# Four-layer transformer block: context maxima, spline stage, last FFN0 stage, ScalarE's order and FFN1's token transposition changed together

## The reference

```python
x = x + tanh(g_xattn[0]) * mlstm(layernorm(x), ctx, ctx, Wi, bi, Wf, bf, ln_scale)   # 16 heads of 32
x = x + tanh(g_ffn[0])   * spline_ffn(layernorm(x), gate_cp, up_cp, down_cp)          # 2048 hidden
x = x + tanh(g_xattn[1]) * attention(layernorm(x), ctx, ctx)                          # 8 heads, over channels
x = x + tanh(g_ffn[1])   * mx_ffn(layernorm(x), gate_w, up_w, down_w)                 # 2048 hidden
```

## Time and profile before

| what | value |
|---|---|
| median of three runs | 1443.43 us |
| the profiled execution's own time | 1442.51 us |
| its span from the first to the last instruction | 1440.4 us |
| TensorE's mean granted clock | 0.932 of full speed |
| busy: PE, DVE, ACT, POOL | 1246.8, 1157.2, 584.2, 367.5 us |
| spline stage, DVE busy / length | 51.4 / 77.1 us |
| FFN0 stages, PE busy / length | 232.3 / 260.5 us |
| FFN1, PE busy / length | 511.4 / 525.4 us |

### The profile page before, as it was taken

One profiled execution on the slowest core, in us unless ns is written; L12 is line 12 of the kernel. 1 busy time (PEld: TensorE's weight loads), 2 busy tenths in 40 slices (PEclk: granted clock), 3 DMA queues, 4 the chain that ended last, 5 costly groups with the idle time before them and its releaser, 6 DMA issues. The chain is left out here.

```text
span 1440.4 us, 18200 instructions
## 1 busy us (share of the span) xinstructions
PE 1246.8 (87%) x6611; PEld 597.2 (41%) x6635; DVE 1157.2 (80%) x1541; ACT 584.2 (41%) x963; POOL 367.5 (26%) x294
## 2 busy tenths in 40 slices
PE   4579999556899898887787888889999999999998
PEld 3258778431343343333122222244444444444444
DVE  6557788875888888888768777888899888889986
ACT  3344665345544444452455645322222322322222
POOL 0031433355433323310367597400000000000000
PEclk8879999675899999998799989999999999999999
DMA  8511033145734263232402304462111121211121
GB/s 292 176 65 61 11 118 118 57 135 179 206 100 135 88 176 88 82 114 83 117 1 64 68 16 87 96 126 51 37 36 36 40 47 39 55 36 36 37 45 44
DMA packets 166561, 122.43 MB, mean 85 GB/s; under 512 B 123855, under 2 KB 134759, under 8 KB 166364
## 3 DMA queue, kind: packets, MB, share of 16 engines
q1 hardware_dynamic: 165212, 117.34, 30.5%
q0 software_dynamic: 1280, 4.20, 1.0%
HBM read 61.15 MB, written 27.66 MB: 62 GB/s over the span
## 5 line engine op out<-in xcount | busy, mean ns | idle before, releaser
L1858 PE MATMUL FD<-W1H,HH 128*128 128x512 f16 x512 | 157.7, 390 | 6.7 <-DVE ROOM L1920 3.6
L2769 PE MATMUL HD<-W1H,HT 128*128 128x512 f16 x480 | 146.5, 382 | 2.5 <-DMA HT<-OS 2.5
L1774 POOL TENSOR_TENSOR HL<-ROOM,HH 128x512 f16<-128x512 f32 x48 | 74.2, 1546 | 168.1 <-ACT HH L1797 168.1
L1852 PE MATMUL FG<-W1L,W1H 97*128 97x512 f16 x324 | 84.3, 385 | 31.9 <-DVE ROOM L1920 14.0
L2534 DVE TENSOR_REDUCE NQ<-A_M 128x2 f32<-128x1024 f32 x60 | 73.3, 1222 | 36.1 <-PE A_M L2382 35.9
L2693 ACT CAST OS<-SS 128x2048 f16<-128x2048 f32 x14 | 26.6, 1899 | 183.9 <-DVEq L2858 183.9
L335 ACT ACTIVATE DD<-E,TM 128x128 f32<-128x128 f32 x256 | 72.9, 370 | 68.4 <-PE E L431 66.8
L1858 PE MATMUL FD<-W1H,HL 128*128 128x512 f16 x256 | 99.4, 388 | 0.0
L2334 ACT ACTIVATE PT<-A_S,CM 128x1024 f32<-128x1024 f32 x64 | 71.2, 1112 | 60.2 <-PE A_S L2408 60.1
L2769 PE MATMUL HD<-W1L,HT 128*128 128x512 f16 x240 | 91.6, 382 | 0.0
L2256 POOL TENSOR_TENSOR SS<-SS,PT 128x512 f32<-128x512 f32 x62 | 83.1, 1360 | 23.8 <-ACT PT L2334 11.3
(11 more groups left out here) (431 smaller groups left out, 2747.8 us busy)
## 6 DMA issues: line engine op xcount, KB each, us to landing
VALP<-in_ffn_weights_dram SPq DMA_DIRECT2D x24, 512.0 KB, 4.1
VALQ<-in_ffn_weights_dram SPq DMA_DIRECT2D x24, 512.0 KB, 4.4
quantised_weights<-QQ SPq DMA_DIRECT2D x24, 512.0 KB, 5.2
X<-in_x_dram SPq DMA_DIRECT2D x8, 1024.0 KB, 6.3
W1L<-features_kept SPq DMA_DIRECT2D x16, 288.0 KB
CTX<-in_ctx_dram SPq DMA_DIRECT2D x4, 1024.0 KB, 7.1
features_kept<-W1L SPq DMA_DIRECT2D x4, 1024.0 KB, 6.0
down_weights<-NAT SPq DMA_DIRECT2D x4, 1024.0 KB, 4.6
```

Source lines behind the costliest of these rows:

```text
L1774: pool.tensor_tensor(HL[:, KI - 1 - i, :], HM[:, i % 2, :], HH[:, i, :], ALU.subtract).then_inc(hl_ready, 1)
L1852: last = pe.matmul(banks[t][:, :], GW[rows, t, lhs, cols], F[b % 2][rows, rhs, c, :], start=(n == 0), stop=(n == 2))
L1858: last = pe.matmul(DN[c][:, :], lhs[:, at, c * P:(c + 1) * P], W2[:, i, part, :], start=(i == 0 and n == 0), stop=(i == KI - 1 and n == 2))
L2769: ins = pe.matmul(DN[:, :], HT[:, lp, i, :], W[:, 2, i * D:(i + 1) * D], start=(i == 0 and lp == 0 and W is WH), stop=(i == KI - 1 and lp ...
```

## The change

Five edits come together.

- **Context maxima.** VectorE reduces each context batch in the mLSTM phase's first loop, four instructions over 128x2048 into columns 3 to 6 of `MXQ`. The library operation that joins the weights' maxima takes seven columns instead of three. GpSimd clamps them afterwards with a `tensor_scalar`. All four batches' scales are formed by four small VectorE instructions at the start of FFN0 (`entry.scales`), and every `top`, `columns`, `largest`, `everywhere` and `scale` of FFN0 and the attention goes, with the three library operations of the attention.
- **Spline stage.** The clearing of `CT` is split between VectorE and GpSimd. ScalarE forms `ln` instead of GpSimd. The first eight units take their slots in `NAT` instead of `WF`, so that ScalarE waits for the added heads (`x_final`) only at unit 8. The units that turn features move from 8 to 11 to 10 to 13, the moments from 14 to 17 to 15 to 18, the last low part to VectorE. SP fetches batch 1's features in FFN0, behind the quantiser's first three loads.
- **FFN0's last stage.** The context is loaded as soon as the last hidden rows are ready, one quantiser tile earlier. The keys move from step 14 to 6 (ScalarE) and 9 (VectorE), batch 1's statistics to step 2, and the queries' low part to GpSimd.
- **ScalarE's order.** In steps that have both, `high` of tile n-1 goes ahead of `bound` of tile n.
- **FFN1.** From tile 3 on the tokens are turned by two transposing DMAs of 128x512 each (high and low part), which SP issues between the two of the hidden tile; TensorE's transpositions and ScalarE's copy of these 13 tiles go.

```diff
@@ spline_phase
-TURN_UNITS = (8, 9, 10, 11)
+TURN_UNITS = (10, 11, 12, 13)
+    def slot(u):
+        if u < CLASS_UNITS:
+            return NAT[0:rows(u), KI - 4 + u % 4, :, :].rearrange("p a d -> p (a d)").bitcast(F32)
+        return WF[0:rows(u), u % 4, :]
...
-                elif k == 8:
-                    features.keep_moments(sp, 1)
-            features.near_elements(sp, 1)
-            features.near_moments(sp, 1)
+            features.keep_moments(sp, 1)
...
-            pool.memset(CT[:, :, :], 0.0).then_inc(ct_zero, 1)
+            pool.memset(CT[:, 1, :], 0.0).then_inc(ct_zero, 1)
             heads = WF[:, :, :]
-            pool.wait_ge(ln_loaded, 16)
-            pool.tensor_scalar(ln, ln, tg[:, 0:1], -1.0, ALU.mult, ALU.mult).then_inc(x_scaled, 1)
...
-            act.wait_ge(x_final, 2)
             for u in range(UNITS_W):
+                if u == CLASS_UNITS:
+                    act.wait_ge(x_final, 2)
...
@@ WeightPeaks
+    def context(self, v, b, ctx):
+        v.tensor_reduce(self.MX[:, 3 + b:4 + b], ctx.rearrange("p c d -> p (c d)"), AX.X, ALU.max,
+                        apply_absolute_value=True).then_inc(self.ctx_max, 1)
...
+        pool.wait_ge(self.ctx_max, B)
         pool.wait_ge(self.mx_ready, 1)
         pool.partition_all_reduce(self.MXA[:, :], self.MX[:, :], P, RMAX).then_inc(self.all_max, 1)
+        pool.wait_ge(self.all_max, 1)
+        pool.tensor_scalar(self.MXA[:, :], self.MXA[:, :], 1e-30, None, ALU.max).then_inc(self.all_max, 1)
@@ FirstBatch
-    def low(self, v):
-        v.wait_ge(self.qh_ready, 1)
+    def low(self, pool):
+        pool.wait_ge(self.qh_ready, 1)
...
-ENTRY = {"deviation": 0, "inverse": 1, "queries": 2, "high": 4, "low": 5, "turn": (7, 9), "values": (8, 10),
-         "top": 11, "columns": 12, "everywhere": 13, "keys": 14}
+ENTRY = {"deviation": 0, "inverse": 1, "queries": 2, "high": 4, "low": 4, "turn": (7, 9), "values": (8, 10),
+         "keys": 6, "keys_low": 9, "statistics": 2}
@@ ffn0_phase
                 quantiser.load(sp, n)
+            features.near_elements(sp, 1)
+            features.near_moments(sp, 1)
...
-                    if s == STAGES - 1 and n == tiles[1]:
+                    if n == sum(STAGE_TILES[0:STAGES - 1]) - 1:
                         sp.wait_ge(hl_ready, B * KI)
...
                     for n in range(Q_TILES):
+                        if ROUNDED_STEP[n] + 1 == at:
+                            quantiser.high(act, n)
+                    for n in range(Q_TILES):
                         if EXPONENT_STEP[n] == at:
                             quantiser.bound(act, n)
-                    for n in range(Q_TILES):
-                        if ROUNDED_STEP[n] + 1 == at:
-                            quantiser.high(act, n)
@@ attention_phase
-                if step == 6 and g % 2 == 1 and b + 1 < B:
-                    scale(b + 1)
...
-            for part in range(2):
-                top(1, part)
-            scale(1)
...
-                if odd:
-                    scale(b + 1)
@@ ffn1_phase
+    PE_TURNED = 3
...
+                    if part == 0 and PE_TURNED <= tt + 2 < TILES:
+                        turned_tokens(tt + 2)
+
+            def turned_tokens(tt):
+                sp.wait_ge(gu_ready, (tt - 1) * IC)
+                for part, ready in enumerate((tokens.xh_ready, tokens.xl_ready)):
+                    sp.wait_ge(ready, tt + 1)
+                    sp.dma_start_transpose(out=XT[tt % 2][:, part, :, :], in_=tokens.XQ[:, part, :]).then_inc(xt_in, 16)
...
-                    pe.wait_ge(xt_taken, tt + 1)
+                    if isinstance(tt, int) and tt < PE_TURNED:
+                        pe.wait_ge(xt_taken, tt + 1)
+                    else:
+                        pe.wait_ge(xt_in, tt * 32 + 32 - 32 * PE_TURNED)
...
-                        if i == IC - 1 and more:
+                        if i == IC - 1 and isinstance(tt, int) and tt + 1 < PE_TURNED:
                             tokens.turn(pe, tt + 1, T[0][:, :, :, :])
```

More of the change, by code:

```diff
@@ L1129, in _ @@
                 t, g = divmod(j, INTER // SUB)
+                if j == 6:
+                    features.transposes(pe, 0, range(0, 2), T)
                 if j >= 6:
@@ L1183, in _ @@
                     features.norm(v, 0, range(NC))
+                    v.wait_ge(ct_zero, 1)
+                if j == 6:
+                    features.low(v, 0, range(0, 2), T)
                 v.wait_ge(ct_high, j + 1)
@@ L2695, in stage @@
                 if gate_up and more:
+                    if not (isinstance(tt, int) and tt + 1 <= PE_TURNED):
+                        act.wait_ge(xt_in, tt * 32 + 32 - 32 * PE_TURNED)
                     tokens.high(act, tt + 1)
                 silu(2)
-                if gate_up and more:
-                    tokens.turned(act, tt + 1, 1 - par, T[0][:, :, :, :])
                 silu(3)
```

187 lines of the change are left out of this document (76 added, 111 removed).

## The result

The changed kernel took 1423.72 us, the median of five runs between 1409.09 and 1424.89, beside 1445.28 us, the median of five runs of the kernel before: a ratio of 0.9845 with a 95% interval from 0.9814 to 0.9876. The forecast was 1410 us with a range from 1394 to 1432. The same kernel was timed twice more in the experiments, on two different chips, with 1412.76 us (0.9816, 0.9799 to 0.9833) and 1412.55 us (0.981, 0.9794 to 0.9826). One run of before, at 1466.53 us, lies outside its fast runs and is left out of the ratios.

The account below looks back on a forecast made before the run. No engine was taken to bound the whole kernel: TensorE bounds FFN1, other phases are largely waits. Terms 2.5 - 8.5 - 2.4 + 0.5 - 5 - 8.5 - 6 - 5.2 = -32.6 us from 1442.5 gave 1410 us, range 1394 to 1432.

Parts of the forecast that it names:

- mLSTM, +2.5: mLSTM phase: early context maxima on VectorE cost +1.5 us and GpSimd's clamp, stalled behind the library operation, +1.
- Spline stage, -8.5: Spline stage: start 4.7 us sooner without the wait for GpSimd's heads, and 3.6 of a 5.48 us wait (0 to -10.9).
- the zero end: Spline stage gains 0 if the loop waits for the heads at unit 8 as long as at unit 0.
- The boundary, -4.8 and +2.4: Batch 1's feature loads leave the spline-FFN0 boundary, -4.8 us; landing late in FFN0 gives half back, net -2.4.
- Scales, +0.5: FFN0's start: the four scale instructions cost +0.5 us (0 to +0.8).
- ScalarE's order, -5: FFN0's full stages: high ahead of bound returns a quarter of TensorE's 20.7 us of waits (+2 to -10).
- FFN0's last stage, -8.5: TensorE loses its context waits, VectorE sets the stage at 53.0 us: -9.5, 1 given back to clock (-4 to -14).
- the 58 that I had named as a sign of being wrong: FFN0's last stage: a length staying above 58 us would show the forecast wrong.
- Attention, -6: Attention: three batches' maxima leave VectorE and 39 us of stalls leave GpSimd, giving -6 us (-1 to -12).
- FFN1, -5.2: FFN1: turning 13 tiles' tokens by DMA instead of TensorE gives net -5.2 us (-5.9 to +25).
- The rival with 4.3 us: FFN1: four-block transfers cost as much as 16-block ones, tokens land 2.4 us late; 1456 us, chance 0.05.
- the one on the next wait taking over: Whole kernel: each chain gives back about half, -15.2 us in all, 1427 us; chance 0.25.

Follow-up runs that it names:

- four_banks: Changed kernel with the second pair of turned value blocks in the two free banks T; 1421.61 us, ratio 0.9839 to the kernel before.
- after_third: The changed kernel a third time, no edit, as comparison for its group; 1412.55 us, ratio 0.981 to the kernel before.
- near_early: Changed kernel with batch 1's features fetched at the spline stage's end again, behind the keeping of the moments; 1419.01 us, ratio 0.9857 to before.
- only_maxima: Kernel before with the context maxima, new FFN0 last stage and attention without maxima; no spline, order or FFN1 part; 1431.96 us, ratio 0.9925.
- heads_late: Changed kernel with GpSimd's four additions of the mLSTM heads held back until VectorE has written all of CT; 1421.53 us, ratio 0.9872 to before.
- no_order: Changed kernel without ScalarE's new order (bound ahead of high as before); 1418.27 us, ratio 0.9869 to the kernel before.
- again: The changed kernel once more, no edit; 1412.76 us, ratio 0.9816 to the kernel before.
- no_ffn1: Changed kernel without its FFN1 part, tokens turned by TensorE on every tile as before; 1417.71 us, ratio 0.9851 to the kernel before.

## Why the prediction was right, and where its steps were not

The time of the profiled execution, 1409.1 us, is that of the forecast, and two of three medians are within 3 us of it. The first median is 14 us above, and its four longer runs have no trace. The one trace of an execution of that length, that of four_banks (1422.96 us), has an mLSTM phase that ends 6.4 us later than in the first trace and a first loop that is 6.4 us longer; that the four runs had the same two is a guess. I did not forecast either.

Part of the agreement is luck. In the two later groups the kernel before ran at 1439.28 and 1440.42 us and not at my 1442.5, so the gain by medians is 26.5 and 27.9 us, and 21.6 in the first group, where my sum says 32.6. In the first trace the phases do add up to that sum, but by errors that cancel: the mLSTM phase came out 5.5 us better than forecast and FFN0 up to its last stage 4.6, the spline stage with its boundary 6.8 worse and the last stage 3.8.

- **mLSTM, +2.5.** Right in size where the clock is alike, as far as two traces tell: +3.2 in after_third (0.74 from 100 to 106 us, before 0.72) and +1.2 in near_early (0.72). In after_third VectorE ends its work 1.5 us later than before, and the clamp holds the barrier for another 2.0 us. VectorE's first instruction of the next phase there:

```profile
288.61 0.91 DVE L1181 MEMSET CT<- 84x1024 uint32 x1 [2.58 <-PEq L163]
```

 The first trace, which alone has the full clock from 90 to 130 us, is 3.0 us shorter than before. A change of phase length under 6 us cannot be read from one trace of this phase.
- **Spline stage, -8.5.** This step failed. The first masked copy comes 22.6 us after GpSimd's first instruction of the stage in both kernels, not 4.7 us sooner. I counted the stall of 8.03 us that leaves the stage as a gain and let every instruction keep its duration. The stall had kept GpSimd's additions away from most of VectorE's float16 copies and norms; without it they run beside each other, and the copies take 4.3 us and the norms 1.7 us longer than alone. only_maxima shows the loss when the stall goes, heads_late shows it gone when the additions are held back. The part behind the first masked copy, for which I had counted 3.6 us, gave 1.2, and that is all that the stage without its boundary gave. The two parts, 4.7 and 3.6, also add up to 8.3 and not to the 8.5 of the sum. I had named the zero end, with another cause for it.
- **The boundary, -4.8 and +2.4.** The boundary, from ScalarE's last cast to FFN0's first product, gave 5.3 us. TensorE waited 0.6 us for the features at most, the loop grew by 0.4, where I had put 2.4.
- **Scales, +0.5.** Inside that 0.4.
- **ScalarE's order, -5.** Right, 6.7 in the trace, 5.5 timed. Of the 6.7 us, 5.3 are TensorE's waits for the product and the silu (20.5 in no_order, 15.2 in again); TensorE is also busy 2.1 us less over the three stages, 205.6 instead of 207.7, at the same mean clock of 0.98. What makes it so is not shown.
- **FFN0's last stage, -8.5.** The mechanism was right, VectorE set it, and the size was off: 4.7 to 5.6. With the bounds of the earlier trace rows the stage is 57.8 us long, just under the 58 that I had named as a sign of being wrong, where I had 53. VectorE's instruction beside GpSimd cost 3.0 us, and TensorE's new wait of 10.3 us for ScalarE's copy of the values, which I had not looked for, made the last product 2.3 us late. But four_banks, without that wait, has no shorter stage: the last store's landing holds it then. ScalarE's copies stand in its order behind quantiser steps that VectorE paces.
- **Attention, -6.** 5.0 to 9.2. The stalls and the maxima are gone as forecast; no run has one of them alone, so how the gain divides between VectorE and GpSimd stays open.
- **FFN1, -5.2.** Right in the whole, of which no_ffn1 gives the turned tokens 4.0 us by its trace and 5.0 by its median; what gave the phase the rest is not shown. TensorE stands up to 0.3 us a tile, but not for the transfers, as I had allowed for: in 11 of the 13 tiles the profile names VectorE's product with up, which ends 0.15 us after the landing. The issues take 1.22 us instead of the 1.0 I had drawn from the longer ones. The estimate from the Trainium skill's page DMA: Bandwidth & Descriptors, 2.5 us to landing, is what the trace shows. The rival with 4.3 us is out.

Of the rivals, the one on the next wait taking over describes the spline stage and half of the last one, though not the sum.

## What to carry to other kernels

Before work is moved to an idle engine, look at what runs beside it in its new place: a VectorE float16 copy, norm or instruction with two SBUF inputs that meets a two-input instruction of GpSimd stands until that has ended, so that moving 2.3 us of work off VectorE cost it 3.0. Short instructions on GpSimd, or a place where VectorE waits anyway, cost less. When a wait is opened, follow the engine that ran ahead to its next wait, through the order of the engine it waits for. And where one kernel's executions lie up to 14 us apart, compare their traces phase by phase before a difference of a few microseconds is put down to an edit.

## What the runs showed of the hardware

- GpSimd stalls 5.8 to 8.5 us ahead of a library operation and 6.7 to 8.0 us ahead of the first `tensor_scalar` or `tensor_tensor` behind it. A memset does not pay, nor does a copy: at 97 us in the profile after a memset and a copy follow `partition_all_reduce` at once, and the first `tensor_tensor` behind them pays 6.72 us. Such a stall can do good, when it keeps GpSimd away from VectorE's instructions.
- VectorE's copy of 20x512 in float16 ends 0.14 to 0.15 us after the GpSimd `tensor_tensor` that it met, and its two-input instruction of 128x1024 1.08 us after, whatever GpSimd's still had to run; a `tensor_tensor` with one input in PSUM is not held.
- A transposing transfer within SBUF of 128x512 in two bytes takes 1.22 us to issue and lands after 2.5; one of 128x2048 takes 1.89 and lands after 4.3.
- The same loop, at the same place, is granted full clock in one execution and 0.68 in another, at a cost of 4.7 us between 91 and 105 us.
- With the DMA engines 96 to 98% busy, FFN0's first loop was 2 to 9 us longer in three executions on one chip, with three engines idle and no semaphore to explain it. Nine traces on other chips do not show it, nor does only_maxima on the same one (28.9 us). What they waited for stays open.
